# Self attention: both additions of the bands on GpSimd, low bands first, product and maximum in one operation per batch

## The reference, cut to what matters

```python
q, k, v = split(x @ W_qkv + b_qkv)
attn = einsum('bsd,btd->bst', q, k) * SCALE
xn   = sigmoid(attn)
mult = where(xn > 0.95, 2.0, where(xn > 0.85, 1.5,
       where(xn < 0.1, 0.1, where(xn < 0.25, 0.3, 1.0))))
attn = softmax(attn * mult, axis=-1)
x    = layernorm(x + (attn @ v) @ W_proj + b_proj)
```

## Time and profile before

| | |
|---|---|
| median of 3 runs | 1484.61 us (1484.57 to 1485.5) |
| the profiled execution's span | 1482.3 us |
| busy, of the span | PE 1369.5 us, DVE 1197.3, POOL 1167.6, ACT 873.4 |
| a step of the self attention (69.48 to 77.00) | 7.52 us |
| busy in that step | DVE 7.13 us, ACT 5.73, PE 5.08, POOL 3.29 |
| granted TensorE clock in that step | 1.00 of full speed |

### The profile page before, as it was taken

The page is one execution under the profiler, slowest core; times in us unless marked ns, Lnnn a source line. Parts: engine busy times, 40 slices in busy tenths (PEclk is TensorE's granted clock), DMA queues, the critical chain, the costliest instruction groups (busy, mean ns, idle before and its releaser), DMA issues. The chain is left out here.

```text
span 1482.3 us, 34966 instructions
## 1 busy us (share of the span) xinstructions
PE 1369.5 (92%) x12862; PEld 1092.1 (74%) x12862; DVE 1197.3 (81%) x2379; ACT 873.4 (59%) x1542; POOL 1167.6 (79%) x1036
## 2 busy tenths in 40 slices
PE   4765699999999977999999999996999999999998
PEld 3554566666666655777777777765999999999997
DVE  5998467766776766888888888886999999999996
ACT  2777444544544534777777777764566666666665
POOL 6344466666666645999999999995999999999997
PEclk8999599999999998999999999999999999999999
DMA  5110343333333305222222222212233233232231
GB/s 157 38 35 27 94 123 94 99 103 105 98 94 94 92 20 171 79 79 79 79 79 78 79 79 78 79 71 69 69 93 88 79 92 87 79 93 86 80 93 29
DMA packets 77195, 123.81 MB, mean 84 GB/s; under 512 B 8354, under 2 KB 45795, under 8 KB 77027
## 3 DMA queue, kind: packets, MB, share of 16 engines
q1 hardware_dynamic: 75426, 117.16, 25.2%
q0 software_dynamic: 1088, 4.19, 1.0%
q10 hardware_dynamic: 512, 0.23, 0.1%
HBM read 70.28 MB, written 51.27 MB: 82 GB/s over the span
## 5 line engine op out<-in xcount | busy, mean ns | idle before, releaser
L971 POOL TENSOR_TENSOR gather_d<-gather_e,gather_rinv 128x1024 f32<-128x1024 f32 x128 | 244.9, 1913 | 44.6 <-DVE gather_rinv L950 44.6
L1230 POOL TENSOR_TENSOR mix_c<-mix_e,mix_rinv 128x1024 f32<-128x1024 f32 x128 | 240.9, 1903 | 17.4 <-DVE mix_rinv L1218 13.4
L1298 PEld LDWEIGHTS last_Y<-kept_phi,last_cT 128*128 128x128 f32 x2048 | 248.3, 192 | 7.1
L1298 PE MATMUL last_Y<-kept_phi,last_cT 128*128 128x128 f32 x2048 | 249.1, 275 | 0.0
L1314 ACT COPY last_cT<-last_T 128x1024 f32<-128x1024 f32 x128 | 128.4, 1003 | 128.8 <-PE last_T L1305 128.8
L1215 DVE TENSOR_REDUCE mix_sums<-mix_e 128x16 f32<-128x1024 f32 x128 | 155.9, 1218 | 32.8 <-ACT mix_e L1189 32.6
L946 DVE TENSOR_REDUCE gather_rsum<-gather_e 128x32 f32<-128x1024 f32 x128 | 156.1, 1220 | 26.2 <-ACT gather_e L919 26.2
L797 POOL TENSOR_TENSOR cross_kd<-first_pack,kept_consts 128x624 fp32r<-128x624 f32 x128 | 155.5, 1236 | 18.9 <-DMA first_pack<-first_halves 12.5
L965 POOL TENSOR_TENSOR gather_dl<-gather_d,gather_dh 128x512 fp32r<-128x512 f32 x128 | 166.2, 1299 | 0.0
L641 ACT ACTIVATE cross_pT<-cross_P 77x1024 f32<-77x1024 f32 x128 | 130.3, 1021 | 49.7 <-PE cross_P L568 49.7
L908 ACT COPY gather_keep<-gather_L 128x256 f32<-128x256 f32 x256 | 94.7, 370 | 104.2 <-PE gather_L L882 97.2
(11 more groups left out here) (195 smaller groups left out, 3166.2 us busy)
## 6 DMA issues: line engine op xcount, KB each, us to landing
kept_logits<-gather_keep SPq DMA_DIRECT2D x128, 256.0 KB, 2.0
mix_read<-kept_logits SPq DMA_DIRECT2D x64, 512.0 KB, 3.7
first_halves<-first_qk SPq DMA_DIRECT2D x32, 412.0 KB, 3.7
first_pack<-first_halves SPq DMA_DIRECT2D x64, 128.0 KB
first_pack<-first_halves SPq DMA_DIRECT2D x32, 206.0 KB
first_pack<-first_halves SPq DMA_DIRECT2D x64, 78.0 KB
attn_xTg<-in_xT SPq DMA_DIRECT2D x16, 256.0 KB, 2.8
kept_xres<-in_x POOLq DMA_DIRECT2D x4, 1024.0 KB, 12.8
```

What stands on the lines that cost most here:

```text
L971: pool.tensor_tensor(dd[u % 4][:].rearrange("p i (n s) -> p i n s", n=16), e[u % 2][:], rinv[u % 2][:].rearrange("p (i n) -> p i n", i=2). ...
L1230: pool.tensor_tensor(self.cc[u % 2][:], self.e[u % 2][:], self.rinv[u % 2][:].unsqueeze(2).to_broadcast([128, 16, EXPERTS]), ALU.mult)\
L1298: ins = pe.matmul(psY[t % 2][:, 0:128], cT[u % 2][:, c, :], w.yk[:, 8 * (u % 2) + c, :], start=(u % 2 == 0 and c == 0), stop=(u % 2 == 1 a ...
```

## The change

GpSimd makes both additions: band[4] as before, then band[5] = band[4] + band[3]. VectorE makes the low bands first (band[1], band[2]), then band[0], and right behind it band[3], which stood after the statistics. The new semaphore `mult_ready` counts the second addition; `top_done` counts band[0], for band[3]'s wait. VectorE's addition, product and maximum are replaced by four operations `tensor_tensor_reduce`, each of which multiplies the 128 columns of one batch and takes their maximum. The first wait of the bands is for `mult_ready` of the group before, in place of `f_ready`.

```diff
@@ GpSimd, group k-1
-                    pool.wait_ge(band_done, 3 * g + 1)
+                    pool.wait_ge(band_done, 2 * g + 1)
                     pool.tensor_tensor(band[4][:], band[1][:], band[2][:], ALU.add).then_inc(low_ready, 1)
+                    pool.wait_ge(band_done, 2 * g + 2)
+                    pool.wait_ge(low_ready, g + 1)
+                    reach(pool, f_ready, g)
+                    pool.tensor_tensor(band[5][:], band[4][:], band[3][:], ALU.add).then_inc(mult_ready, 1)
@@ VectorE, group k-1, at the start of the step
                     dve.wait_ge(a_ready, g + 1)
-                    reach(dve, f_ready, g)
+                    reach(dve, mult_ready, g)
                     av = a[g % 2][:]
-                    dve.tensor_scalar(band[0][:], av, T_095, 2.0, ALU.is_gt, ALU.add)
                     dve.tensor_scalar(band[1][:], av, T_025, -1.4, ALU.is_lt, ALU.mult)
                     dve.tensor_scalar(band[2][:], av, T_01, -0.4, ALU.is_lt, ALU.mult).then_inc(band_done, 1)
+                    dve.tensor_scalar(band[0][:], av, T_095, 2.0, ALU.is_gt, ALU.add).then_inc(top_done, 1)
+                    dve.wait_ge(top_done, g + 1)
+                    dve.scalar_tensor_tensor(out=band[3][:], in0=av, scalar=T_085, in1=band[0][:],
+                                             op0=ALU.is_gt, op1=ALU.add).then_inc(band_done, 1)
@@ VectorE, group k-1, after the statistics of group k-3
-                    dve.wait_ge(band_done, 3 * g + 1)
-                    dve.scalar_tensor_tensor(out=band[3][:], in0=av, scalar=T_085, in1=band[0][:],
-                                             op0=ALU.is_gt, op1=ALU.add).then_inc(band_done, 1)
-                    dve.wait_ge(band_done, 3 * g + 2)
-                    dve.wait_ge(low_ready, g + 1)
-                    dve.tensor_tensor(band[5][:], band[4][:], band[3][:], ALU.add).then_inc(band_done, 1)
-                    dve.wait_ge(band_done, 3 * g + 3)
+                    dve.wait_ge(mult_ready, g + 1)
                     reach(dve, p_ready, g - 1)
-                    dve.tensor_tensor(f2[g % 2][:], band[5][:], av, ALU.mult).then_inc(f2_done, 1)
-                    dve.wait_ge(f2_done, g + 1)
-                    dve.tensor_reduce(mx[:], f2[g % 2][:].rearrange("p (b t) -> p b t", b=GB), X, ALU.max)\
-                       .then_inc(mx_done, 1)
+                    for b in range(GB):
+                        c = slice(b * 128, (b + 1) * 128)
+                        ins = dve.tensor_tensor_reduce(out=f2[g % 2][:, c], in0=band[5][:, c], in1=av[:, c], scale=1.0,
+                                                       scalar=-FILL, op0=ALU.mult, op1=ALU.max, accum_out=mx[:, b:b + 1])
+                    ins.then_inc(mx_done, 1)
```

More of the change, by code:

```diff
@@ L189, in attention @@
         (u_made, v_made, s_made, uT_ready, v_ready, rb_ready, a_ready, f_ready, p_ready, pT_made, pT_ready,
-         o_made, mv_ready, rstd_ready, shift_ready, x1_ready, x1T_made, x1T_kept, low_ready, band_done, f2_done,
+         o_made, mv_ready, rstd_ready, shift_ready, x1_ready, x1T_made, x1T_kept, low_ready, mult_ready, band_done, top_done,
          mx_done, y_chain, pool_chain) = (
@@ L194, in attention @@
                                 "rstd_ready", "shift_ready", "x1_ready", "x1T_made", "x1T_kept", "low_ready",
-                                "band_done", "f2_done", "mx_done", "y_chain", "pool_chain"))
+                                "mult_ready", "band_done", "top_done", "mx_done", "y_chain", "pool_chain"))
         fill_made, row_set = st.sem("fill_made"), st.sem("row_set")
```

## The result

The changed kernel takes 1488.66 us (median of 7 runs, 1486.89 to 1489.54), the kernel before 1484.64 (7 runs, 1482.53 to 1485.68). The ratio is 1.0025, 95% interval 1.0014 to 1.0035: slower by 2.1 to 5.2 us. The forecast was 1488.2.

The account below looks back on a forecast made before the run. VectorE's queue was taken to bound the self-attention stage; +4.3 (steps 4 to 15), -1.25 (step 3) and +0.55 (step 16) gave +3.6 us, so 1488.2 us with the difference to the median added; range 1484.3 to 1494.

Parts of the forecast that it names:

- L387 meets the first addition and ends 0.55 behind it: Middle steps: band[3], moved behind band[0], stands still until GpSimd's addition ends, ending at 2.80; `rb` starts 1.70 us later.
- `rb`, `vp` and `y` are not held up beside the second addition: Middle steps: these VectorE operations run beside GpSimd's second addition at no cost; waiting would add 1.4 us a step.
- `rstd` becomes late: Middle steps: last `mv` comes at 6.16, so `shift` waits for GpSimd's `rstd` until 7.71, making a step 7.88 us.
- a wait of 0.3 to 0.6: Sign in the changed profile: VectorE waits 0.3 to 0.6 us for `rstd` before `shift`, where there was no wait.
- The fused operations cost about 1.0 and are hidden: Middle steps: four fused operations at 0.25 to 0.3 us each, hidden up to 1.48 us by the wait for `rstd`.
- So the fusion buys nothing: Middle steps: fusing product and maximum saves no time, since `shift` waits for `rstd` anyway.
- Step 3: Early step where `rb` waits for TensorE's V, so L387's delay falls into an existing wait: -1.25 us.
- over 1 us shorter: Sign in the changed profile: Step 3 becomes over 1 us shorter.
- Step 16: Last step, with no successor's bands; its `nb` comes later, adding +0.55 us.
- Twelve steps: Middle steps 4 to 15, each 0.36 us longer: +4.3 us.
- The rival of the lock kept for the whole of `rstd`: Middle steps: GpSimd keeps the ports throughout `rstd`, delaying the last two fused operations; step 8.12, +7.0 us, 1491.6; chance 0.10.
- The later chain follows step 16's `nb`, and later stages cost nothing: Stage end and after: ScalarE's and the later chain follow that `nb`; later stages cost nothing, 0.5 us either way.

Follow-up runs that it names:

- e9: Changed kernel with GpSimd's first addition made to wait for band[3] as well; 1476.31 us, ratio 0.9938 to the kernel before.
- e3: Changed kernel with GpSimd's first addition on 256 of 512 columns, second reading band[1] for band[4] (computation incomplete); 1480.88 us, ratio 0.9973 to the kernel before.
- e4: Changed kernel with product and maximum again as two operations of 512 columns; 1493.84 us, ratio 1.0061 to the kernel before.
- e6: Changed kernel with `shift` moved from ahead of `nb` into the next step, behind band[2]; 1484.06 us, ratio 0.9992 to the kernel before.
- e7: Changed kernel with bands ordered 0, 1, 3, 2, first addition behind them, and `shift` in the next step behind the bands; 1467.65 us, ratio 0.9886.

## Why the prediction was right, point by point

The mechanism in the middle steps was right, in its parts and in size. That the time of the whole kernel was hit within 0.5 us is in part luck (point 9).

1. *VectorE's queue is the bound of the stage.* Right: every step length in the table is VectorE's queue plus what it stands still.
2. *L387 meets the first addition and ends 0.55 behind it.* Right in place and size: 1.64 for the 1.6 to 1.7 forecast, in all middle steps, shown by e9 and e3. Also right that a one-input band holds GpSimd up in turn: the addition takes 1.38 instead of 1.27; I had its end at 2.25 into the step, it is at 2.21.
3. *`rb`, `vp` and `y` are not held up beside the second addition.* Right: 0.67 and 1.13.
4. *`rstd` becomes late.* Right: idle time 0.69 before `shift`, at 7.67 into the step (forecast 7.71); `rstd` took 1.15, that is 0.14 of contention for my 0.15. The sign that I had given, a wait of 0.3 to 0.6, was just missed, since the fused operations end at 6.98 and not at about 7.1.
5. *The fused operations cost about 1.0 and are hidden.* The cost is right (75.53 to 76.47, 0.94 in all, one every 0.19 to 0.25). *So the fusion buys nothing* is wrong: it buys 0.22 (e4). I had written that VectorE's two-input operations hold GpSimd up, and did not apply it to the product that the fusion replaces.
6. *Step 3 gives 1.25 back.* It gave 0.92, and the sign "over 1 us shorter" did not come. The stretch from `rb` to the next step is 5.18, as worked out (5.17), but `rb` came 0.43 late, not 0.1: step 3 could not start before 38.11, when ScalarE had `a` ready, and 2.70 of bands and stall run past the 40.38 at which TensorE's V had been there.
7. *Step 16: +0.55*, measured +0.50. *Twelve steps: +4.3*, measured +3.90. The sum of +3.6 against +3.48 owes a little to two errors of opposite sign, in points 6 and 7.
8. The rival of the lock kept for the whole of `rstd` fell: the third and fourth fused operation run inside `rstd` at 0.28.

9. *The later chain follows step 16's `nb`, and later stages cost nothing, with 0.5 either way.* Both wrong. The sum took VectorE's delay to be the stage's; SyncE, whose queue I had left out of the path, ends the stage, and passed on 2.1 of the 3.48 in the profiled executions. The later stages took 3.1 us longer there. The medians differ by +4.0, so that some 1.9 of it does not come from the start of the next stage, if that start is taken from the profiles; no run shows its cause. The two errors have opposite signs, and the +3.6 of the sum is near +4.0 by that luck. The +3.48 on VectorE's own queue is no luck but for points 6 and 7.

## What to carry to other kernels

Work that is moved to GpSimd must be placed by what VectorE does at that time. In this kernel an addition of 512 columns was free beside operations that read PSUM (`vp` 0.67 to 0.69, `y` 1.13) and beside the statistics (0.87). Beside an operation with two SBUF inputs, or beside a band (`tensor_scalar` on one SBUF tensor), one of the two stood still until the other was done. It does not follow from "one SBUF input": the statistics (beside an addition) and the maximum (L397 of e4, beside `rstd`) have one, too, and neither they nor GpSimd stood still. What sets the bands apart is not shown. A wait that keeps GpSimd's operation back can make the kernel faster. Before VectorE's work is shortened, look for what it covered: here the 2.67 us between the statistics and `shift` hid a round trip over GpSimd, and the shortened queue just waited for it; moving the reader of the round trip into the next step brought the gain that the shortening had promised. Shorter two-input operations are worth something even on an engine that waits, if they let the other engine in sooner (0.22 a step in e4). And a delay on the busiest engine is only worth its length at the stage's end if that engine's chain ends the stage: look at what opens the barrier, here SyncE's issues.

## What the runs showed of the hardware that I had not expected

- A fused product and maximum over 128 float32 columns takes 0.28 us with a read of its accumulator of 0.08 beside it, and four of them follow each other every 0.21 to 0.22 us on the mean: cheaper than two operations of 512 columns (1.41) by a third.
- The engines take turns: in the changed kernel band[0] goes first, the addition second, band[3] third, in steps 2 to 16; a 4-column operation put in between (e6) changed the turns and made the one-input band wait 1.08 us.
- GpSimd's power of 4 columns takes 1.01 alone, 1.15 beside the fused operations and 1.41 in e7, where the next step's bands begin while it runs; in none of these rows does it hold a VectorE operation up by its own length (bands 0.42 to 0.43, fused operations 0.28).
